# Routing merged with the expert loop, its one-hot tables in bf16, and the weight loads reordered, in a two-stage attention and mixture-of-experts kernel

## The reference

```python
def _L0_attn_ref(x, ...):          # 16 heads, second-order Taylor features of q and k, causal,
    ...                            # plus 128 encoder keys; normaliser z; output projection Wout
x = L0_attn_x
x = _layernorm(x + _L0_attn_ref(x, ...))

def _L0_ffn_ref(hidden_states, w1, b1, w2, b2, wr, br):
    x = hidden_states.reshape(-1, h)                  # 4096 tokens x 256
    logits = x @ wr + br                              # 8 experts
    probs = softmax(logits)
    top_p, top_i = top_k(probs, 2)
    gate = top_p[:, 0] / (top_p[:, 0] + top_p[:, 1])  # of the best two
    for e in range(8):                                # only the best expert of a token counts
        hout = gelu(x @ w1[e] + b1[e]) @ w2[e] + b2[e]
        out = out + where((top1 == e)[:, None], hout * gate[:, None], 0.0)
x = _layernorm(x + _L0_ffn_ref(x, ...))
```

## Time and profile before

| what | us |
|---|---|
| median of three runs (1138.42 to 2505.81) | 1139.74 |
| profiled execution, its own time | 1140.3 |
| its span in the profile | 1138.5 |
| attention block | 0 to about 788 |
| routing block | about 788 to 814.5 |
| experts block | about 814.5 to 1138.5 |
| TensorE busy, over the span | 1043.6 (92%) |
| VectorE, ScalarE, GpSimd busy | 539.5, 507.5, 477.2 |

### The profile page before, as it was taken

The page is one execution under the profiler, slowest core; times in us unless marked ns, Lnnn a source line. Parts: engine busy times, 40 slices in busy tenths (PEclk is TensorE's granted clock), DMA queues, the critical chain, the costliest instruction groups (busy, mean ns, idle before and its releaser), DMA issues. The chain is left out here.

```text
span 1138.5 us, 19845 instructions
## 1 busy us (share of the span) xinstructions
PE 1043.6 (92%) x6944; PEld 694.9 (61%) x6945; DVE 539.5 (47%) x923; ACT 507.5 (45%) x892; POOL 477.2 (42%) x507
## 2 busy tenths in 40 slices
PE   5799999999999999999999999994379999999995
PEld 4344455546546545555654654564269999998984
DVE  5385763582573456357357356775502222222222
ACT  2566644653663564465356356330033333333331
POOL 1265543353443444336344244430114555555553
PEclk9799999999999999999999999997589999999998
DMA  5732641651563254265156236113844555554430
GB/s 205 280 109 100 202 143 64 200 190 53 181 178 106 89 191 143 65 201 198 43 180 188 96 107 177 39 38 123 342 173 144 175 184 183 183 180 161 165 105 2
DMA packets 59255, 167.56 MB, mean 147 GB/s; under 512 B 7246, under 2 KB 11344, under 8 KB 52914
## 3 DMA queue, kind: packets, MB, share of 16 engines
q1 hardware_dynamic: 55442, 157.32, 41.3%
q0 software_dynamic: 3744, 9.31, 2.6%
HBM read 120.24 MB, written 47.29 MB: 147 GB/s over the span
## 5 line engine op out<-in xcount | busy, mean ns | idle before, releaser
L381 ACT ACTIVATE w<-slot 128x1024 f32<-128x1024 f32 (+1 forms) x256 | 230.9, 915 | 181.3 <-PE slot L756 181.1
L515 DVE SCALAR_TENSOR_TENSOR w<-w,mask 128x256 f32<-128x256 f32 (+1 forms) x192 | 180.2, 938 | 188.1 <-ACT w L381 177.2
L777 PE MATMUL osum<-w,values 128*64 128x512 f32 (+3 forms) x1280 | 252.4, 490 | 1.9 <-DVE w L518 1.9
L348 POOL TENSOR_TENSOR wsum<-w 128x512 f32<-128x512 f32 x64 | 96.2, 1504 | 366.6 <-DVE w L518 366.6
L352 POOL TENSOR_TENSOR wsum<-wsum,w 128x768 f32<-128x768 f32 x64 | 123.4, 1929 | 63.6 <-DVE w L518 61.8
L1252 PEld LDWEIGHTS up<-rowsT,w 128*128 128x128 f32 x1248 | 147.5, 194 | 3.6 <-issue 1.7
L1252 PE MATMUL up<-rowsT,w 128*128 128x128 f32 x1248 | 147.9, 277 | 1.1 <-ACT rowsT L1180 1.1
L1240 PE MATMUL down<-w,active 128*128 x624 | 144.8, 386 | 2.1 <-issue 1.8
L518 DVE TENSOR_SCALAR w<-w 128x768 f32<-128x768 f32 (+2 forms) x192 | 138.4, 721 | 0.0
L756 PE MATMUL slot<-qop,kop 64*128 64x512 f32 (+3 forms) x640 | 126.3, 425 | 9.1 <-issue 6.9
L1240 PEld LDWEIGHTS down<-w,active 128*128 128x128 f32 x624 | 116.7, 192 | 20.2 <-issue 4.6
(11 more groups left out here) (205 smaller groups left out, 1080.8 us busy)
## 6 DMA issues: line engine op xcount, KB each, us to landing
w<-in_w SPq DMA_DIRECT2D x47, 1024.0 KB, 4.9
kop<-k_rows SPq DMA_DIRECT2D x32, 640.0 KB, 5.8
qop<-q_rows SPq DMA_DIRECT2D x32, 512.0 KB, 7.2
inv<-inv_rows SPq DMA_DIRECT2D x56, 256.0 KB, 4.5
k_rows<-kh SPq DMA_DIRECT2D x32, 320.0 KB
k_rows<-kl SPq DMA_DIRECT2D x32, 320.0 KB
q_rows<-qh SPq DMA_DIRECT2D x32, 256.0 KB
q_rows<-ql SPq DMA_DIRECT2D x32, 256.0 KB
```

The source lines that it names most:

```text
L348: pool.tensor_tensor(dst[:, 0, :], src[:, 0, 0:N], src[:, 0, N:2 * N], ALU.add)
L381: act.activation(w[:, n % 2, :, at:at + cols], slot[u % 2][:, :, 0:cols], ACT.Square, bias=HALF_ROOT).then_inc(squared, 1)
L515: dve.scalar_tensor_tensor(src[:, :, 0:cut], src[:, :, 0:cut], 0.5, mask[:, 0:cut].unsqueeze(1).to_broadcast([P, 2, cut]), ALU.add, ALU.mu ...
L777: last = pe.matmul(osum[n % 2][HD * s:HD * s + HD, q0:N], values[:, j, h * HD:h * HD + HD], w[:, n % 2, s, at:at + N - q0], start=(u == 0) ...
```

## The change

The two blocks `route` and `run_experts` become one, `route_and_run`; the meeting of the engines between them is gone, and waits on new semaphores stand in its place: `listed` (the row list is there; GpSimd waits for it before gather 0), `known` (the experts of the slots are there; SyncE, ScalarE and TensorE wait for it), and `routed` (gates and output list are there; GpSimd waits for it ahead of finish(0), TensorE ahead of the first down).

`in_slot`, `in_row` and `carried` become bf16. A token number does not fit in bf16, so `carried` holds two parts: the token tile's number (0 to 31) and the number within the tile plus one (1 to 128); VectorE puts them together after the sum (`token_f`). The gate is held in three bf16 parts and summed in a second pass of 32 matmuls of its own (`carried_gate`, `gate_found`), which VectorE feeds after the row list and the expert list are out. Three of the eight chunks of `in_row` are made by ScalarE (Square of the difference, then Relu of one minus that). The position arithmetic on VectorE is two instructions shorter. The sums take the PSUM banks of `down`.

SyncE loads six of the eight w2 ahead, then waits for `known`, fetches w1 for slot 0, waits until gather 0 has landed, fetches w1 for slot 1, then loads the last two w2 (TensorE waits for them ahead of the second down), then fetches for slots 2 and 3.

The diff, cut to what differs in the work (the lists of VectorE, TensorE and SyncE move into the new function otherwise unchanged):

```diff
+BY_DVE, BY_ACT = [0, 1, 2, 3, 4], [5, 6, 7]
+EARLY_W2 = 6
...
-    in_slot = sb("in_slot", [P, TT, EVEN])
-    carried = sb("carried", [P, TT, 3, EVEN], F32R)
-    in_row = sb("in_row", [P, TT, P], F32R)
+    in_slot = sb("in_slot", [P, TT, EVEN], BF16)
+    carried = sb("carried", [P, TT, 2, EVEN], BF16)
+    carried_gate = sb("carried_gate", [P, TT, 3, EVEN], BF16)
+    in_row = sb("in_row", [P, TT, P], BF16)
+    apart = sb("apart", [P, TT // CODED, P])
...
+    row_found, gate_found = down[0][:, 0:2 * EVEN], down[1][:, 0:3 * EVEN]
...
     @block.sync
     def _(sp):
+        sp.dma_start(b1[:, :], b1_in).then_inc(table_loaded, 16)
+        sp.dma_start(b2[:, :], b2_in.partition_broadcast(P)).then_inc(table_loaded, 16)
+        for e in range(EARLY_W2):
+            sp.dma_start(w2[:, e, :, :], w2_in[:, e, :, :]).then_inc(w2_full, 16)
+        sp.wait_ge(known, 1)
...
         for s in range(FETCHED):
+            if s == 1:
+                sp.wait_ge(gathered[0], 16)
             fetch(s, s)
+            if s == 1:
+                for e in range(EARLY_W2, E):
+                    sp.dma_start(w2[:, e, :, :], w2_in[:, e, :, :]).then_inc(w2_late, 16)
...
         pool.wait_ge(ready_consts, 2)
+        pool.wait_ge(listed, 1)
...
         for s in range(3):
             gather(s, s)
 
+        pool.wait_ge(routed, 1)
         finish(0, 0)
         gather(3, 3)
...
+        act.wait_ge(exp_in, 1)
+        act.activation(gate[:, :], second[:, :], ACT.Exp).then_inc(exp_out, 1)
+        act.wait_ge(rows_of, 1)
+        for i, c in enumerate(BY_ACT):
+            n_t = TT // CODED
+            if i > 0:
+                act.wait_ge(placed_act, i)
+            for j in range(n_t):
+                t = c * n_t + j
+                act.activation(apart[:, j, :], count128[:, :], ACT.Square, bias=row_f[:, t:t + 1],
+                               scale=-1.0).then_inc(apart_made, 1)
+            act.wait_ge(apart_made, n_t * (i + 1))
+            act.activation(in_row[:, c * n_t:(c + 1) * n_t, :], apart[:, :, :], ACT.Relu, bias=1.0,
+                           scale=-1.0).then_inc(placed_act, 1)
+        act.wait_ge(table_loaded, 32)
+        act.wait_ge(known, 1)
...
+        pe.wait_ge(carried_ready, 2)
...
+            last = pe.matmul(row_found, in_row[:, t, :], carried[:, t, :, :].rearrange("p a s -> p (a s)"),
+                             start=(i == 0), stop=(i == TT - 1))
+        last.then_inc(found_rows, 1)
+        pe.wait_ge(carried_gate_ready, 3)
+        for t in range(TT):
+            last = pe.matmul(gate_found, in_row[:, t, :], carried_gate[:, t, :, :].rearrange("p a s -> p (a s)"),
+                             start=(t == 0), stop=(t == TT - 1))
+        last.then_inc(found_gates, 1)
+        pe.wait_ge(known, 1)
...
             if isinstance(s, int) and s == 0:
+                pe.wait_ge(w2_full, 16 * EARLY_W2)
+                pe.wait_ge(routed, 1)
+            if isinstance(s, int) and s == 1:
+                pe.wait_ge(w2_late, 16 * (E - EARLY_W2))
...
-        after(dve.tensor_scalar(first_row[:, :], first_row[:, :], float(P), None, ALU.mult))
-        after(dve.tensor_tensor(place[:, :, :], cum[:, :, :].rearrange("p e t -> p t e"), by_tile, ALU.subtract))
-        after(dve.tensor_tensor(place[:, :, :], place[:, :, :], ranks[:, :].rearrange("p (t e) -> p t e", e=E),
-                                ALU.add))
-        after(dve.tensor_tensor(place[:, :, :], place[:, :, :], over_t(first_row[:, :]), ALU.add))
+        after(dve.tensor_tensor(place[:, :, :], cum[:, :, 0:TT].rearrange("p e t -> p t e"),
+                                ranks.rearrange("p (t e) -> p t e", e=E), ALU.add))
+        after(dve.scalar_tensor_tensor(place[:, :, :], over_t(first_row[:, :]), float(P), place[:, :, :], ALU.mult,
+                                       ALU.add))
...
+        dve.sem_inc(rows_of, 1)
         after(dve.tensor_tensor(in_slot[:, :, :], ...
+        dve.tensor_tensor(carried[:, :, 0, :], in_slot[:, :, :], tile_no[:, :].unsqueeze(2).to_broadcast([P, TT, EVEN]),
+                          ALU.mult).then_inc(carried_ready, 1)
+        dve.tensor_scalar(carried[:, :, 1, :], in_slot[:, :, :], token_no[:, 0:1], None,
+                          ALU.mult).then_inc(carried_ready, 1)
+        for c in BY_DVE:
...
+                              ALU.is_equal).then_inc(placed, 1)
+        dve.wait_ge(exp_out, 1)
+        after(dve.tensor_scalar(gate[:, :], gate[:, :], 1.0, None, ALU.add))
+        after(dve.reciprocal(gate[:, :], gate[:, :]))
+        for k in range(3):
+            after(dve.tensor_copy(gate_parts[:, k, :], gate[:, :]))
+            if k < 2:
+                after(dve.tensor_tensor(gate[:, :], gate[:, :], gate_parts[:, k, :], ALU.subtract))
+        dve.wait_ge(found_rows, 1)
+        after(dve.tensor_copy(token_f[:, :], row_found[:, EVEN:EVEN + SLOTS]))
+        after(dve.scalar_tensor_tensor(token_f[:, :], row_found[:, 0:SLOTS], float(P), token_f[:, :], ALU.mult, ALU.add))
+        after(dve.tensor_copy(row_index[:, :], token_f[:, :]))
+        dve.sem_inc(listed, 1)
+        after(dve.tensor_tensor(slots_past[:, :, :], ...
+        after(dve.tensor_reduce(expert_f[:, :], slots_past[:, :, :], AX.X, ALU.add))
+        after(dve.tensor_copy(expert_of[:, :], expert_f[:, :]))
+        dve.sem_inc(known, 1)
+        for k in range(3):
+            dve.tensor_tensor(carried_gate[:, :, k, :], in_slot[:, :, :],
+                              gate_parts[:, k, :].unsqueeze(2).to_broadcast([P, TT, EVEN]),
+                              ALU.mult).then_inc(carried_gate_ready, 1)
+        after(dve.tensor_scalar(empty[:, :], token_f[:, :], 0.0, float(SKIP + 1), ALU.is_equal, ALU.mult))
+        after(dve.scalar_tensor_tensor(index_f[:, :], token_f[:, :], -1.0, empty[:, :], ALU.add, ALU.add))
+        after(dve.tensor_copy(out_index[:, :], index_f[:, :]))
+        dve.wait_ge(found_gates, 1)
+        after(dve.tensor_copy(gates[:, :], gate_found[:, 0:SLOTS]))
+        for k in (1, 2):
+            after(dve.tensor_tensor(gates[:, :], gates[:, :], gate_found[:, k * EVEN:k * EVEN + SLOTS], ALU.add))
+        dve.sem_inc(routed, 1)
+        dve.wait_ge(table_loaded, 32)
```

More of the change, by code:

```diff
@@ L856, in experts, with route_and_run @@
         table_loaded = sem("table_loaded")
[L857 to L864, removed]
+        w2_full, w2_late = sem("expert_w2_loaded"), sem("last_w2_loaded")
+        known, listed, routed = sem("experts_known"), sem("rows_listed"), sem("routed")
+        route_and_run(nc, ctx, sem, table_loaded, w2_full, w2_late, known, listed, routed, w1, w2, b1, b2, w1_in, w2_in, b1_in,
+                      b2_in, logits, tables, row_index, out_index, gates, expert_of, ybuf, ident, out)
 EVEN = SLOTS + SLOTS % 2
-CODED = 8
+BY_DVE, BY_ACT = [0, 1, 2, 3, 4], [5, 6, 7]
+CODED = len(BY_DVE) + len(BY_ACT)
 FETCHED = 4
-def route(nc, ctx, sem, table_loaded, w2_full, routed, w2, b1, b2, w2_in, b1_in, b2_in,
-          logits, tables, row_index, out_index, gates, expert_of):
+EARLY_W2 = 6
+def route_and_run(nc, ctx, sem, table_loaded, w2_full, w2_late, known, listed, routed, w1, w2, b1, b2, w1_in, w2_in, b1_in,
+                  b2_in, logits, tables, row_index, out_index, gates, expert_of, ybuf, ident, out):
+    RING = 4
+    UNROLL = 4
+    PEELED = 3
     falling, tile_starts, count128, before, ones, ones32 = tables
@@ L920, in route @@
     placed = sem("placed")
[L921 to L999, removed]
-        after(dve.tensor_scalar(first_row[:, :], first_row[:, :], float(P), None, ALU.mult))
-        after(dve.tensor_tensor(place[:, :, :], cum[:, :, :].rearrange("p e t -> p t e"), by_tile, ALU.subtract))
-        after(dve.tensor_tensor(place[:, :, :], place[:, :, :], ranks[:, :].rearrange("p (t e) -> p t e", e=E),
-                                ALU.add))
-        after(dve.tensor_tensor(place[:, :, :], place[:, :, :], over_t(first_row[:, :]), ALU.add))
[L1006 to L1025, removed]
-            tiles = slice(c * n_t, (c + 1) * n_t)
-            dve.tensor_tensor(in_row[:, tiles, :], count128[:, :].unsqueeze(1).to_broadcast([P, n_t, P]),
-                              row_f[:, tiles].unsqueeze(2).to_broadcast([P, n_t, P]),
-                              ALU.is_equal).then_inc(placed, 1)
-        after(dve.tensor_tensor(passed[:, :, :], count128[:, 0:SLOTS].unsqueeze(2).to_broadcast([P, SLOTS, E - 1]),
-                                last_slot[:, 0:E - 1].unsqueeze(1).to_broadcast([P, SLOTS, E - 1]), ALU.is_ge))
-        after(dve.tensor_reduce(expert_f[:, :], passed[:, :, :], AX.X, ALU.add))
-        after(dve.tensor_copy(expert_of[:, :], expert_f[:, :]))
-        dve.wait_ge(found_all, 1)
-        after(dve.tensor_copy(row_index[:, :], found[:, 0:SLOTS]))
-        after(dve.tensor_copy(gates[:, :], found[:, EVEN:EVEN + SLOTS]))
-        after(dve.tensor_tensor(gates[:, :], gates[:, :], found[:, 2 * EVEN:2 * EVEN + SLOTS], ALU.add))
```

(12 more changed lines are left out.)

133 lines of the change are left out of this document (95 added, 38 removed).

## The result

The changed kernel takes 1130.38 us (median), the kernel before 1139.12 in runs on the same chips: a ratio of 0.9924, 95% interval 0.9910 to 0.9939, so 8.7 us or 0.8% faster. The interval tells this from no change, though the prediction had put the limit at about 2%. One execution of each kernel (2505.81 and 3399.32 us) was a slow one and is not in the ratio. The forecast was 1132.4, inside a range from 1127.5 to 1138.5. The profiled execution of the changed kernel took 1132.74 us, with a span of 1131.0.

The account below looks back on a forecast made before the run. The prediction took the start of up(0) to set the end, held by VectorE's list, the turn of the blocks and gather 0 among w1; 1140.3 - 7.3 = 1133.0, less 0.56 to the median: 1132.4, range 1127.5 to 1138.5.

Parts of the forecast that it names:

- the limit at about 2%: About 2% (23 us) was what a measurement of this kernel could tell from no change; same was given 0.95.
- Position arithmetic and tables: VectorE's routing: arithmetic 0.66 us shorter, `row_f` ending at 797.31; two-input tables 1.49 us, one-input table 0.8.
- ScalarE's chunks: Three chunks of `in_row` on ScalarE, some 2.0 us each, all before VectorE's last chunk; price nothing.
- The sums: TensorE's first pass at 0.11 us a bf16 matmul, ending about 804.8; `listed` at 806.65, 6.6 us earlier.
- rival B: The bf16 matmuls keep 0.221 us, bound by instruction rate or weight load: 5.9 us less gain, 1138.3; chance 0.10.
- The gather: Gather 0, issued after the index copy at 806.7, meets empty queues and lands in about 2.8 us, at 810.6.
- one to three tables: By the skill's port rule, VectorE's gate tables delay gather 0 by up to 4.5 us, to 815.1.
- rival C: Gather 0 starves until VectorE is idle after the gates at 816.7; up(0) at 821.9, total 1137.1; chance 0.08.
- What is late next: TensorE's second pass, behind three gate tables, ends at 815.95 ahead of `turn`; up(0) at 817.2, 7.3 us sooner.
- holding the weights back costs nothing: Slot 1's w1 fetch, held until gather 0 lands, arrives at 816.9, well ahead of up(1); 6 us of slack.
- D: Slower than before: TensorE's loop step lengthens from 7.37 to 7.70 us over 31 steps, 1142.6; chance 0.07.
- A: Tables run at double pace and the clock is already up at up(0): 11.6 us gained, 1128.1; chance 0.13.

Follow-up runs that it names:

- e2: The changed kernel with its four tables in fp32 and fp32r instead of bf16; ratio to the kernel before 0.9988, logits to up(0) 36.01 us.
- e5: The changed kernel with VectorE's three gate tables held until gather 0 has landed; ratio to the kernel before 0.9972, gather 0 landing in 5.3 us.
- e9: The changed kernel with slot 0's w1 fetch held until gather 0 has landed, one execution; gather 0 landed in 4.2 us, logits to up(0) 32.61 us.
- e10: The changed kernel with slot 0's w1 fetch and the gate tables held until gather 0 has landed, one execution; gather 0 took 3.0 us.
- e6: The changed kernel without gate tables and second pass, every gate 1.0; ratio to the kernel before 0.9914, logits to up(0) 27.24 us.
- e3: The changed kernel with all eight w2 loaded ahead and slot 1's w1 fetch not held for gather 0; ratio to the kernel before 0.9911.
- e12: The changed kernel with gather 3 ahead of finish(0), all eight w2 loaded ahead and no hold of slot 1's fetch; ratio to the kernel before 0.9852.
- e4: The changed kernel with gather 3 issued right behind gather 2, ahead of finish(0); ratio to the kernel before 0.9860.
- e11: The changed kernel with fp32r tables, and gather 0 and the first w1 fetch released at the routing's end; ratio to the kernel before 1.0053.
- e1: The changed kernel with gather 0 and the first w1 fetch released only at the end of the whole routing; ratio to the kernel before 0.9996.
- e7: The changed kernel with gather 3 ahead of finish(0), gate tables held for gather 0, second pass behind up(1); ratio to the kernel before 0.9888.

## Why the prediction held, point by point

**Position arithmetic and tables.** Forecast 9.76 us from the logits to the end of `row_f`, measured 9.85. The one-input table took 0.55 us where I took 0.8. By the rule of the Trainium skill ("VectorE: DVE Perf Modes", What auto-detection actually checks) I had estimated 0.5 for it, and the trace agrees with the page there, and for the gate tables too, which stayed near the fp32 price of 1.49 us, at 1.43 each. ScalarE's chunks took 1.28 + 0.63 us, forecast 2.0; TensorE waited 0.69 us for the third one, which the gate's arithmetic on VectorE hid as said.

**The sums.** Forecast 0.11 us a matmul, measured 0.078 and 0.106. e2 shows what the upper end would have cost: 6.8 us, I had 5.9 for rival B. The row list was forecast 19.10 us behind the logits and came at 18.97.

**The gather.** This step failed: "gather 0 meets empty queues and lands in about 2.8 us". It took 6.1. e5, e9 and e10 show that the w1 fetch for slot 0 alone adds 2.3 us to 3.0 and VectorE's tables alone 1.2. My own sum issues that fetch 1.4 us behind the gather, while the gather is under way, and then leaves it out of the gather's price. On the tables the Trainium skill ("SBUF — State Buffer", SBUF: two separate sides) points the right way: it says that a VectorE instruction with two inputs in SBUF and a GpSimd instruction that reads SBUF lock each other out. The trace agrees that the tables hold the gather up: GpSimd's issue took 2.43 us beside them and 1.21 without. But the page speaks of starved descriptors, on which I went, only for VectorE's two-port modes, and the price was 1.2 us, not one to three tables; it is about what was left of the first table when the issue began (807.54 + 1.43 - 807.69 = 1.28).

I also misread, which I set against the rule there and in rival C. The VectorE instruction begins at 862.61 and the issue ends at 861.67 + 1.01 = 862.68, so they meet for 0.07 us only, and the row says nothing either way. What does run beside that instruction is GpSimd's copy behind the issue, and it took 0.45 us where the same copy without such company takes 0.20. The two copies in the kernel before:

```profile
862.68 0.45 POOL L1145 COPY out_col<-out_index 128x1 int32 x1
...
869.89 0.20 POOL L1145 COPY out_col<-out_index 128x1 int32 x1
```

So the trace of the kernel before had the sign already. The miss of 3.3 us cost nothing, since the prediction had the second pass end some 5 us behind the gather (815.95 against 810.6), and it still ended 1.5 us behind it; but it left only 2.0 us to be had from that pass, which e6 shows.

**What is late next.** TensorE's own list, as forecast: the pass ended 28.13 us behind the logits (forecast 28.40), up(0) began at 29.22 (forecast 29.65). The gain up to up(0) was 7.70 us against 7.3. The prediction had it that holding the weights back costs nothing, which held; that it also brings nothing at the end was not in it (it gave the gather empty queues for it), and is what e3 and e12 show.

**The rivals.** B, C and D did not come about: the matmuls are twice as fast, up(0) came forward, and the loop step is 7.40 us, far from 7.61. Of A, the tables ran at the slow pace; the clock was up at up(0) in the profiled executions of e3, e4 and e12, and not in that of the changed kernel (below). What I had not seen is that taking away the early release or the bf16, either one, takes nearly the whole gain, because the second pass is new work: e11 without both is slower than the kernel before.

## What to carry to other kernels

Before a step is made faster, look for what else holds the same end: here a swap of one line, gather 3 ahead of finish(0), brought 7 us on either kernel, nearly as much as the whole change (8.7). A merged block pays through the transfers that it lets start before the last result; if it also brings new work on the path, cost that work alone, as its own change. A transfer's price from a quiet place holds only if nothing else is issued beside it: count what the same release sets free, on the other queues and on the other engines (here VectorE's tables).

## What was not expected of the hardware

The clock at up(0) differs between executions with the same work ahead of it. In the changed kernel TensorE began the second pass at 811.89 and the granted clock rose only in 820 to 822. In e4, with the same pass from 811.22, it rose in 814 to 816. Windows of the changed kernel (length, busy us of each engine, granted clock, DMA share, GB/s):

```profile
818.00:820.00 2.00, 2.00 (x11) 2.00 (x11) 0.00 (x0) 0.00 (x0) 0.00 (x0) 0.50 1.03 434
820.00:822.00 2.00, 2.00 (x17) 2.00 (x17) 0.00 (x0) 0.00 (x0) 0.00 (x0) 0.83 0.99 418
```

And of e4:

```profile
814.00:816.00 2.00, 1.35 (x11) 0.98 (x10) 0.59 (x3) 0.38 (x1) 1.21 (x3) 0.72 0.66 152
816.00:818.00 2.00, 2.00 (x21) 2.00 (x20) 0.00 (x0) 0.00 (x0) 0.12 (x1) 1.00 1.01 426
```

up(0) took 5.86 us in the one and 3.81 in the other, a difference of 2.05 us that the edit does not explain; it was 3.81 in e3 and e12 as well, and over 5.2 in all other profiled executions. Part of the spread of single runs goes with the clock: of the changed kernel's runs, the four with a mean granted clock of 0.967 took 1124.46 to 1128.98 us, the four at 0.962 or less 1132.74 to 1135.98. That mean covers the whole span, so it does not say that up(0) is the place; what decides when the clock rises stays open, and no run here tells it. The profiled executions of the two kernels both have a mean of 0.961; over all runs the changed kernel's median is 0.964, and the kernel before had 0.960 in the runs beside e1 to e4. So some part of the 8.7 us, above the 7.5 of the profiled pair, may be the clock; that is not shown. The 0.3% between e4 and e7, which their intervals do not settle, may be the clock too (6.41 us against 3.81 in their profiled executions); that was not settled either.
